# Two small GpSimd operations move from the start of a stage to between the three operations that split q and k

## The reference

```
x = x + attention(layernorm(x), ctx)      # q, k with rotary angles; window of 65 keys
x = x + experts(layernorm(x))
```

```
logits = xf @ router_w.T;  k_probs, k_idx = top_k(softmax(logits), 2)
buf[flat_e, slot] += xf[token_id]                     # slots by order of arrival, up to a capacity
out_buf = einsum(silu(einsum(buf, w1)), w2)
combined = sum(out_buf[flat_e, slot] * k_probs) + x   # x here is the normalised input of the experts
```

## Time and profile before

| | |
|---|---|
| median of 3 runs | 537.87 us (535.21 to 539.02) |
| the profiled execution | 535.63 us, span 533.8 us |
| mean granted clock of TensorE | 0.897 |
| busy share of the span | PE 76%, DVE 64%, POOL 62%, ACT 49% |
| instructions on POOL | 282 |

### The profile page before, as it was taken

The page is one execution under the profiler, slowest core; times in us unless marked ns, Lnnn a source line. Parts: engine busy times, 40 slices in busy tenths (PEclk is TensorE's granted clock), DMA queues, the critical chain, the costliest instruction groups (busy, mean ns, idle before and its releaser), DMA issues.

```text
span 533.8 us, 16115 instructions
## 1 busy us (share of the span) xinstructions
PE 406.4 (76%) x5587; PEld 317.7 (60%) x5587; DVE 341.9 (64%) x1062; ACT 263.7 (49%) x587; POOL 332.7 (62%) x282
## 2 busy tenths in 40 slices
PE   3463598899989989998999737799998878886100
PEld 2242466677767767776777623588887766765000
DVE  4785377698989888988888440477865545634100
ACT  1110355355665555664556520588987677564000
POOL 7442033288777777787665885028768687686683
PEclk9766799899999999999999958799999999989555
DMA  8987796688877888988985335336455554342331
GB/s 188 230 215 166 194 235 160 170 174 185 206 164 177 172 186 187 204 180 163 186 180 102 47 31 109 115 98 125 71 118 84 116 75 81 30 39 26 29 35 15
DMA packets 89045, 70.31 MB, mean 132 GB/s; under 512 B 8992, under 2 KB 75808, under 8 KB 88480
## 3 DMA queue, kind: packets, MB, share of 16 engines
q1 hardware_dynamic: 68208, 60.09, 44.1%
q0 software_dynamic: 20784, 9.53, 19.7%
HBM read 38.85 MB, written 30.74 MB: 130 GB/s over the span
## 4 chain that ended last, share of the span: by engine, by line
POOL 26%; SPq 20%; PE 20%; DMA 15%; issue 14%; DVE 2%; ACT 1%; POOLq 0%; DVEq 0%; ACTq 0%
POOL out L1428 17%; PE bank L470 17%; POOL queues L1337 6%; SPq L369 5%; DMA out<-ys,row_token 4%; DMA k_scratch<-parts 4%; SPq L367 4%; SPq L349 4%; SPq L354 3%; DMA q_pack<-maxT 3%; DMA k_pack<-k_scratch 1%; SPq L379 1%; DVE xn L960 1%; POOL base L1373 1%; DMA xs<-queues 1%
## 5 line engine op out<-in xcount | busy, mean ns | idle before, releaser
L1428 POOL DMA_INDIRECT out<-ys,row_token x80 | 125.2, 1565 | 69.5 <-issue 48.9
L918 DVE TENSOR_REDUCE maxima<-bank 128x4 f32<-128x512 f32 x128 | 87.3, 685 | 40.1 <-PE bank L470 37.7
L1337 POOL DMA_INDIRECT queues<-rows,index x64 | 100.3, 1567 | 16.7 <-issue 16.0
L781 ACT ACTIVATE probs<-bank 128x512 f32<-128x512 f32 x128 | 76.4, 597 | 55.4 <-PE bank L470 54.1
L470 PE MATMUL bank<-xTp,w1p 128*128 128x512 f32 (+1 forms) x288 | 65.6, 379 | 12.4 <-DVE xTp L1179 12.4
L470 PE MATMUL bank<-k_pack,q_pack 128*64 128x128 bf16 x1024 | 54.6, 232 | 18.5 <-DMA k_pack<-k_scratch 17.8
L470 PE MATMUL bank<-q_pack,k_pack 128*128 128x64 bf16 x1024 | 53.1, 196 | 15.3 <-DMA q_pack<-maxT 14.4
L1287 DVE TENSOR_TENSOR hidp<-hid,hidp 128x512 fp32r<-128x512 f32 (+1 forms) x96 | 55.7, 600 | 13.3 <-ACT hidp L893 12.0
L470 PEld LDWEIGHTS bank<-xTp,w1p 128*128 128x128 f32 x288 | 49.6, 198 | 22.5 <-DVE xTp L1179 14.5
L470 PE MATMUL bank<-hidp,w2p 128*128 128x512 f32 (+1 forms) x288 | 62.2, 364 | 0.0
L889 ACT ACTIVATE hid<-bank 128x512 f32<-128x512 f32 (+1 forms) x96 | 53.1, 553 | 17.5 <-PE bank L470 17.4
(11 more groups left out here) (138 smaller groups left out, 678.2 us busy)
## 6 DMA issues: line engine op xcount, KB each, us to landing
k_pack<-k_scratch SPq DMA_DIRECT2D x64, 192.0 KB, 4.1
q_pack<-q_scratch SPq DMA_DIRECT2D x64, 128.0 KB, 3.2
queues<-empty SPq DMA_DIRECT2D x8, 682.5 KB, 7.4
xs<-queues SPq DMA_DIRECT2D x7, 650.0 KB
q_scratch<-parts SPq DMA_DIRECT2D x16, 192.0 KB
k_scratch<-parts SPq DMA_DIRECT2D x16, 192.0 KB
xin<-in_x SPq DMA_DIRECT2D x16, 128.0 KB, 3.1
cin<-in_ctx SPq DMA_DIRECT2D x16, 128.0 KB, 3.6
```

What stands on the lines that cost most here:

```text
L781: nc.scalar.activation(probs[u % 2][:], bb[u % 2][:], ACT.Exp).then_inc(S["prob_s"], 1)
L918: v.reduce_max(maxima[par][:, 4 * hg:4 * hg + 4, i2], ab[u % 2][:].rearrange("p (h c) -> p h c", c=P), AX).then_inc(S["max_s"], 1)
L1337: g.indirect_dma_start(queues, bass.IndirectOffsetOnAxis(ap=index[par][:, n:n + 1], axis=0), rows[par][:, n // TILES, n % TILES, :], None, ...
L1428: g.indirect_dma_start(out, bass.IndirectOffsetOnAxis(ap=row_token[par][0:n, t:t + 1], axis=0), ys[c][0:n, col // P, :], None, compute_op= ...
```

## The change

In the stages in which both batch k - 2 and batch k + 3 exist (2 to 12), `token_numbers` moves behind `qk` and `base_of_output` behind `rest`; the wait for the normalised rows moves with `token_numbers`. In stages 13 to 17, where nothing is split any more, the order is as before.

```diff
-                if on(k - 2):
+                splitting = on(k + 3)
+                if on(k - 2) and not splitting:
                     after(pool, "xn2_s", 2, k - 2)
                     apart(pool, "past_pool")
                     if not last_steps:
...
                     g.tensor_tensor(qk[:], straight[:], turned[:], ALU.add).then_inc(S["qk_s"], 1)
+                    if on(k - 2):
+                        after(pool, "xn2_s", 2, k - 2)
+                        apart(pool, "past_pool")
+                        token_numbers(par)
                     after(pool, "part1", 1, k + 3)
                     after(pool, "part2", 1, k + 2)
                     g.tensor_tensor(rest[:], qk[:], parts[:, 0, :, :], ALU.subtract).then_inc(S["rest_s"], 1)
-                if on(k + 3):
+                    if on(k - 2):
+                        base_of_output()
                     after(pool, "part2", 1, k + 3)
                     g.tensor_tensor(parts[:, 2, :, :], rest[:], parts[:, 1, :, :], ALU.subtract).then_inc(S["part3"], 1)
```

## The result

The changed kernel takes 574.8 us (median of 4 runs, 571.5 to 578.3) against 537.4 us: 1.0715 times as long, 95% interval 1.0665 to 1.0764. That is 37.4 us more by the medians and 38.4 by the ratio. The forecast was 567 with a range of 548 to 580. The profiled execution took 576.7 us, with a span of 574.9.

A forecast was written before the change was run, and what follows sets the result against it. SyncE's queue and TensorE were taken to set the pace together. Loop 22.5 us plus clock 7.6 us gave 30.1 on the profiled 535.6, 565.7; with the runs' median 2.2 us higher, 567 was said, range 548 to 580.

The forecast's parts named there:

- What is removed: Base and token numbers leave their place ahead of qk on GpSimd: 0.83 us a stage, buying nothing as qk waits for VectorE.
- What is put between the three operations: On GpSimd, token numbers (0.15 us) and base (0.70 us) go into waits for ScalarE around rest, costing GpSimd nothing.
- The stop in SyncE's queue: SyncE arrives 1.6 us too early for the base's DMA and stands still, holding the maxima queued behind it.
- the loop through the maxima and unit 4: Maxima, unit 4, rotated k, qk, rest, base, SyncE's DMA, next maxima: 17.82 us a stage against 15.93, 22.5 us in all; 88%.
- The leg of 10.6 us: From SyncE's base DMA to TensorE's next unit 4: taken as 10.6 us, from eight legs of 10.11 to 11.98, mean 10.99.
- The clock: TensorE idles about 2.5 us before unit 4, so its clock may fall: 1.51 us a stage, half of ten taken, 7.6 us.
- the row of stage 2: Before the change, stage 2 idled 1.91 us, then ran at clock 0.50: unit 4 to rest took 7.90 us, not 6.39.
- The sizes of the signs: Expected in the changed profile: line 399 waits of 1.5 to 2.5 us each; TensorE's waits for maxima 20 to 30 us.
- a clock that falls in each stage: Variant of the closed loop in which TensorE's clock falls in every stage: 575 us.
- the stop paid once: Rival: SyncE's base wait eats its wait for landed parts, TensorE takes up the rest; 1.6 to 2 us, 540; 6%.
- GpSimd's relief: Rival: qk follows GpSimd, not VectorE, so 0.83 us in eleven stages come off, 9.1 us, 527 to 529; 3%.
- the new place is reached: Denies the rival that the new order isn't reached because the loop's k is no number: 538 us; 1%.

The follow-up runs named there:

- after_late_dma: The changed kernel with the base's DMA issued one stage later, where SyncE waits for the parts anyway, and the loop begun at stage 4: 533.9 us.
- sp_wait_only: The kernel before, with SyncE alone also waiting for rest of batch k + 3 ahead of the base's DMA in stages 2 to 12: 560.4 us.
- after_pe_busy: The changed kernel plus twelve unread products of 384 columns on TensorE ahead of its wait for the maxima in stages 2 to 12: 561.4 us.
- sp_wait_part3: The kernel before, with SyncE also waiting for the third part of batch k + 3 ahead of the base's DMA in stages 2 to 12: 589.4 us.
- tokens_only: Against the kernel before, only the token numbers move behind qk; the base stays ahead of qk: 535.4 us, ratio 0.997.

## Why the prediction was right, by its steps

- What is removed buys nothing: right. qk starts 0.15 us behind rotated k in the rows above, with 3.6 us of idle time ahead of it.
- What is put between the three operations costs GpSimd nothing: right. The third part starts at 165.17, 0.08 us behind the base; the token numbers alone measured 0.997. The base does hold VectorE up, but by less than the 0.7 us that the prediction allowed for: line 932's operation ends with it (165.12 against 165.09) and takes 0.33 to 0.41 us beside it in the eleven stages, where the same operation takes 0.16 to 0.18 us nearly everywhere else. The longer one, "index" (1.02 us), ends with rest (164.46 against 164.44) and not with the base; in the kernel before it took 0.71 to 1.07 us in ten of the eleven stages as well. None of this is the loss: after_late_dma keeps GpSimd's changed order and takes no longer than the kernel before.
- The stop in SyncE's queue, and the loop through the maxima and unit 4: right, shown from both sides by sp_wait_only and after_late_dma. Its terms, predicted and measured in the changed kernel: unit 4 to the end of rest at the full clock 6.39 and 6.38 us; the base 0.70 and 0.65 (164.44 to 165.09); its release 0.13 and 0.19; from SyncE's DMA to the next unit 4 10.6 and a mean of 10.8 (eleven legs, from 108.70 to 119.63 first and 303.42 to 313.78 last). Together 17.82 and, in after_pe_busy, where the clock doesn't fall, 17.96 a stage (100.09 to 279.66 for ten). The loop's share of the whole was put at 22.5 us and is 22 to 24. The leg of 10.6 us is partly a choice: of the eight legs averaged in the prediction, one (to 163.68) ends in a wait that the row calls issue and not maxima; without it their mean is 11.01 us.
- The clock: the right mechanism, mis-sized. I took 7.6 us, half of ten falls of 1.51 us each. It fell in seven of the ten stages, and cost 14.2 us in the trace (the ten ways from unit 4 to rest above, less 6.39 each) and 13.4 to 16 us by the timings of after_pe_busy. Three falls (stages 6, 8 and 10) cost 1.36 to 1.46 us, as the row of stage 2 had said; the other four cost 2.45 to 2.58 us. In those the clock was already low when unit 4 began: its first eight products took 0.61 us and not 0.41, as at 119.63 and 232.33 against 158.06. The prediction reckoned that an early fall would lie partly in the idle time and cost less. A part did lie there (118.9 to 119.63 in stage 3), but the low stretch went on until 125.7, 6.1 us behind unit 4's start; in stage 6 the whole of it, 176.9 to 180.3, was 3.4 us. Why it lasts longer in some stages, the runs do not show.
- The sizes of the signs were too low for the same reason. SyncE's waits at line 399 came to 3.6 us each, where 1.5 to 2.5 were expected, and TensorE's waits to 33.1 us, where 20 to 30 were; in after_pe_busy, at the full clock, SyncE's ten are 1.95 us each.
- Some of the closeness is luck. The measured 574.8 is what the prediction gave for a clock that falls in each stage (575); it fell in seven, and four of these falls cost more than was reckoned.
- What is left of the difference: stage 2's unit 4 came at 100.18 in this execution and at 99.01 before, ahead of anything that the change could touch; in the traces of the other kernels it lies between 97.16 and 100.09.
- The rivals: the stop paid once (540) fell with sp_wait_part3; GpSimd's relief (527 to 529) did not appear in tokens_only (535.4); the new place is reached, eleven times.

## What to carry to other kernels

An operation that goes into a free gap on its own engine can still be the release of a DMA, and then its old, early place was what kept a DMA queue from stopping. Follow its semaphore to the queue that waits on it, see when that queue arrives there, and ask what is queued behind: here an output that nobody was in a hurry for held the input for which TensorE waited. Put DMAs of results behind those that others wait for, best where the queue has to wait for a landing anyway.

## What the runs showed of the hardware that was not expected

The length of TensorE's idle time alone does not say whether the clock falls: in the changed kernel it fell in stages with 2.34, 2.51, 2.79 and 3.09 us of it, and not in stages 4, 7 and 5 with 2.38, 2.40 and 2.86 us.

What a fall costs the loop goes by how much of the low stretch lies behind TensorE's return, not by how early it begins. In the changed kernel 3.4 us behind it cost 1.46 us (stage 6), and 6.1 us cost 2.51 (stage 3). Two stages of sp_wait_part3 show falls that begin still earlier (stretches as above, then unit 4):

```profile
196.40:203.10 6.70, 5.72 (x57) 3.58 (x55) 3.70 (x14) 0.85 (x2) 2.46 (x3) 0.50 0.74 173
237.40:240.70 3.30, 2.95 (x29) 1.71 (x23) 1.94 (x9) 0.25 (x1) 2.47 (x3) 0.50 1.16 270
```

```profile
199.50 0.61 PE L473 MATMUL bank<-q_pack,k_pack 128*128 128x64 bf16 x8 [0.98 <-DMA q_pack<-maxT]
...
241.57 0.41 PE L473 MATMUL bank<-q_pack,k_pack 128*128 128x64 bf16 x8 [1.22 <-DMA q_pack<-maxT]
```

In the first, some 3.7 us of the low stretch lie behind unit 4, and the way to the end of rest took 7.99 us, 1.60 more than at the full clock; in the second it is over before unit 4 begins, and the way took 6.38 us. So each microsecond of the low clock behind the return cost about 0.4 us here.

Twelve idle products of 384 columns, 2.12 us of TensorE's time in each of eleven stages, gave 13 to 16 us back.
